# Segment sums of a graph network scanned and stored chunk by chunk, with one row per partition mended at the end

## What is computed

```python
def spline_conv(x, edge_index, basis, wi, weight, root, bias):   # twice, each behind elu
    msg = sum over s of basis[:, s, None] * xW[src, wi[:, s]]
    out = jax.ops.segment_sum(msg, dst, num_segments=n)
    deg = jax.ops.segment_sum(jnp.ones((dst.shape[0],)), dst, num_segments=n)
    out = out / jnp.clip(deg, 1.0)[:, None]
    return out + x @ root + bias

for l in range(3):                                               # layer 3
    e = edge_attr @ We[l] + be[l]
    msg = jax.nn.relu(x[src] + e)
    agg = jax.ops.segment_sum(msg, dst, num_segments=n)
    x = jax.nn.leaky_relu((x + agg) @ W[l] + b[l], negative_slope=0.01)
```

## Time and profile before

| | us |
|---|---|
| median of three runs | 7850.94 |
| profiled execution, own time | 7858.02 |
| its span | 7856.2 |
| DVE busy | 4300.7 (55%) |
| POOL busy | 5213.5 (66%) |
| PE busy | 2708.5 (34%) |
| ACT busy | 1275.8 (16%) |

### The profile page before, as it was taken

One profiled execution on the slowest core, in us unless ns is written; L12 is line 12 of the kernel. 1 busy time (PEld: TensorE's weight loads), 2 busy tenths in 40 slices (PEclk: granted clock), 3 DMA queues, 4 the chain that ended last, 5 costly groups with the idle time before them and its releaser, 6 DMA issues. The chain is left out here.

```text
span 7856.2 us, 39070 instructions
## 1 busy us (share of the span) xinstructions
PE 2708.5 (34%) x8375; PEld 1703.4 (22%) x8375; DVE 4300.7 (55%) x7258; ACT 1275.8 (16%) x2189; POOL 5213.5 (66%) x5106
## 2 busy tenths in 40 slices
PE   0000000005323300287745552776233365365222
PEld 0000000003211100133323332554133133233111
DVE  6999979921244700255548887778666422322311
ACT  0000000001111200276621010111244011011000
POOL 4777778887777277775567772663477476476477
PEclk9999999966555655698867776777555555555555
DMA  1111110013333000112212221221344222222111
GB/s 45 24 31 27 26 23 19 18 21 104 98 51 49 13 23 23 30 43 53 47 40 42 42 41 46 33 33 23 79 78 75 56 39 37 57 40 35 59 35 30
DMA packets 364618, 331.80 MB, mean 42 GB/s; under 512 B 115499, under 2 KB 339968, under 8 KB 363379
## 3 DMA queue, kind: packets, MB, share of 16 engines
q0 software_dynamic: 163072, 77.69, 11.5%
q1 hardware_dynamic: 199282, 249.37, 9.6%
q10 hardware_dynamic: 2048, 2.41, 0.1%
HBM read 173.11 MB, written 158.67 MB: 42 GB/s over the span
## 5 line engine op out<-in xcount | busy, mean ns | idle before, releaser
L889 POOL DMA_INDIRECT c_ring<-tab,QB x784 | 762.6, 973 | 614.5 <-POOLq L102 298.9
L889 POOL DMA_INDIRECT g_ring<-tab,QB x784 | 743.3, 948 | 420.4 <-issue 238.4
L889 POOL DMA_INDIRECT l_ring<-in_x_dram,a_own x392 | 538.4, 1373 | 130.9 <-issue 119.2
L1338 POOL DMA_INDIRECT nodes<-l1s_rowr,a_out x392 | 386.2, 985 | 264.3 <-DVE l1s_rowr L1354 145.1
L2007 POOL DMA_INDIRECT out_dram<-out_rowr,out_idxr x392 | 386.4, 986 | 221.9 <-issue 123.3
L1461 PE MATMUL c_psU<-spline,c_hzT 96*128 96x288 f32 x1568 | 516.8, 477 | 40.5 <-DVE c_V L1425 40.2
L889 POOL DMA_INDIRECT sort_ring<-in_x_dram,sort_raw x392 | 412.7, 1053 | 120.5 <-issue 119.2
L889 POOL DMA_INDIRECT l_ring<-agg_tab,QA x392 | 401.7, 1025 | 135.3 <-issue 119.2
L889 POOL DMA_INDIRECT H<-xe_tab,idx_a x392 | 406.0, 1036 | 122.6 <-issue 118.9
L889 POOL DMA_INDIRECT rows_b<-b_edges,idx_b x392 | 399.4, 1019 | 130.5 <-issue 118.9
L889 POOL DMA_INDIRECT c_ring<-nodes,b_other x392 | 386.9, 987 | 128.7 <-issue 118.0
(11 more groups left out here) (480 smaller groups left out, 8291.5 us busy)
## 6 DMA issues: line engine op xcount, KB each, us to landing
tab<-M SPq DMA_DIRECT2D x5, 6272.0 KB
nodes<-l_xout SPq DMA_DIRECT2D x40, 322.3 KB
nodes_x<-nodes SPq DMA_DIRECT2D x50, 257.8 KB
c_din<-dst_lin SPq DMA_DIRECT2D x98, 128.0 KB, 2.8
c_ring<-tab,QB POOLq DMA_INDIRECT x784, 3.3
dst_lin<-c_yd SPq DMA_DIRECT2D x98, 128.0 KB
g_din<-dst_lin SPq DMA_DIRECT2D x98, 128.0 KB, 2.8
g_ring<-tab,QB POOLq DMA_INDIRECT x784
```

Source lines behind the costliest of these rows:

```text
L889: pool.indirect_dma_start(out=ring[:, at + j, :], out_offset=None, in_=table, in_offset=bass.IndirectOffsetOnAxis(ap=idx[:, w:w + 1], axis ...
L1338: pool.indirect_dma_start(out=g.nodes2, out_offset=bass.IndirectOffsetOnAxis(ap=A.out[:, w:w + 1], axis=0), in_=rowr[k % NR][:, j, :], in_ ...
```

## The change

Nothing of what the reference computes is changed. Six edits:

1. **Scan within the stage.** A class `Segments` replaces `M`. The messages of chunk c go to a tile `T` of 128 x 32 x 9, feature by feature; column 0 takes the running sum of the chunk before (`open`), and two scans of 144 elements, 16 features each, sum the chunk (`scan`), with flags `B.run` laid out in the same form (made by ACT during c1). ACT copies `T` back to row order (`flatten`), and SP stores the chunk to the table (`keep`).
2. **Mending.** The sums of a partition's first segment lack what comes from the partitions before. Only the last row of that segment in each partition is used by the index lists, so at a stage's end one indirect DMA gathers 128 rows, DVE adds the carry (`close`), and one indirect DMA scatters them back (`mend`). `close_segments` is gone.
3. **The destination side** is loaded from the table by SP, chunk by chunk (128 KB each), in c2, c3, g0, g1 and out. In c2 and c3 it lands in the second half of `ring`, so that two additions of 256 elements become one of 512; the SP load then also waits for `tn.used`.
4. **Degree and bias.** `inv` goes into the spline's weights in `Basis`; the bias is a 97th row of the spline's weight matrix, against a row of ones in `hzT`. 18 small DMAs load it.
5. **The degree** is made in `l1s` instead of in layer 0, spread to every edge of a segment, along with the row numbers for the mending (`degrees`, `seams`), behind the eighth chunk.
6. Five tables instead of two, with their extra row stored in `l1s`.

```diff
 def load_weights(g, a):
+            bias = a["L2_gnn_b1"] if c == 0 else a["L2_gnn_b2"]
+            for j in range(9):
+                loads.append((g.spline[c][3 * D:3 * D + 1, j, :], bias.unsqueeze(0)))
 def layer0_edges(...):
-            link(v.memset(inv[:, :, :], 1.0))
-            scan_sum(g, v, link, ci, 0, inv, B, 1)
-            link(v.reciprocal(inv[:, :, :], inv[:, :, :]))
 def layer1_rest(...):                     # phase l1s, DVE
+            def degrees():
+                notlast = first
+                link(v.memset(count[:, :, :], 1.0))
+                scan_sum(g, v, link, ci, 0, count, B, 1)
...
+                carry_dve(v, link, cb, 0, [count[:, 0, :]], [sfx[:, 0:1]], back=True)
...
+                link(v.reciprocal(inv[:, :, :], count[:, :, :]))
             for k in range(g.NCH):
                 cols = slice(k * CH, (k + 1) * CH)
+                if k == 2 * NR:
+                    degrees()
+                    seams()
-def close_segments(g, B, M, table, ph_name, scale=None, bias=None):
...
+class Segments:
+    def into(self, c):
+        return self.T[c % self.n][:, :, 1:CH + 1].rearrange("p f w -> p w f")
+
+    def open(self, v, link, c):
+        if c >= self.n:
+            v.wait_ge(self.flat, c - self.n + 1)
+        if c == 0:
+            link.inc(v.memset(self.T[0][:, :, 0], 0.0))
+        else:
+            v.wait_ge(self.summed, 2 * c)
+            link.inc(v.tensor_copy(self.T[c % self.n][:, :, 0], self.T[(c - 1) % self.n][:, :, CH]))
+
+    def scan(self, v, link, c):
+        v.wait_ge(link.sem, link.base + link.n)
+        on = self.B.run[:, c, :, :].rearrange("p f w -> p (f w)")
+        for h in range(2):
+            t = self.T[c % self.n][:, h * (D // 2):(h + 1) * (D // 2), :].rearrange("p f w -> p (f w)")
+            v.tensor_tensor_scan(t, on, t, 0.0, ALU.mult, ALU.add).then_inc(self.summed, 1)
+
+    def flatten(self, act, c):
+        act.wait_ge(self.summed, 2 * (c + 1))
+        if c >= 2:
+            act.wait_ge(self.kept[c % 2], 16 * (c // 2))
+        act.copy(self.rows[c % 2][:, :, :], self.into(c)).then_inc(self.flat, 1)
+
+    def keep(self, sp, c):
+        sp.wait_ge(self.flat, c + 1)
+        sp.dma_start(lin(self.g, self.table[0:self.g.NP, :], c), self.rows[c % 2][:, :, :]).then_inc(self.kept[c % 2], 16)
+
+    def close(self, v, link):
+        g, last = self.g, self.T[(self.g.NCH - 1) % self.n]
+        v.wait_ge(self.summed, 2 * g.NCH)
+        carry_dve(v, link, self.c, 0, [last[:, :, CH]], [self.B.pfx[:, g.W - 1:g.W].broadcast_to([P, D])])
+        v.wait_ge(self.fetched, 16)
+        v.tensor_tensor(self.ends[:, :], self.ends[:, :], self.c.carry[:, :], ALU.add).then_inc(self.fixed, 1)
+
+    def mend(self, pool):
+        g, B = self.g, self.B
+        for i in range(2):
+            pool.wait_ge(self.kept[i], 16 * ((g.NCH + 1 - i) // 2))
+        pool.indirect_dma_start(out=self.ends[:, :], out_offset=None, in_=self.table,
+                                in_offset=bass.IndirectOffsetOnAxis(ap=B.get[:, 0:1], axis=0)).then_inc(self.fetched, 16)
+        pool.wait_ge(self.fixed, 1)
+        pool.indirect_dma_start(out=self.table, out_offset=bass.IndirectOffsetOnAxis(ap=B.put[:, 0:1], axis=0),
+                                in_=self.ends[:, :], in_offset=None, bounds_check=g.NP - 1, oob_is_err=False).then_inc(self.put, 16)
+        pool.wait_ge(self.put, 16)
 class Spline:                             # weigh, DVE
         times(0)
         times(1)
+        self.seg.open(v, link, c)
         add(0)
...
         add(3)
+        v.wait_ge(self.added, 4 * (c + 1))
+        self.seg.scan(v, link, c)
 def conv2_edges(...):
-                gather_from(g, pool, table, QB, ring[c % NR], c, 0, got[c % NR])
+                gather_from(g, pool, table, QB, ring[c % NR], c, 0, got[c % NR])
+            seg.mend(pool)
             def load(c):                  # SP
                 if c >= NR:
                     sp.wait_ge(tn.turned, c - NR + 1)
+                    sp.wait_ge(tn.used, c - NR + 1)
                 sp.dma_start(din[c % NR][:, :, :], lin(g, g.dst_lin, c)).then_inc(dgot[c % NR], 16)
+                sp.dma_start(ring[c % NR][:, CH:N2, :], lin(g, table[0:g.NP, :], c)).then_inc(mgot[c % NR], 16)
             def store(c):                 # SP
                 sp.wait_ge(new, c + 1)
                 sp.dma_start(lin(g, g.dst_lin, c), yd[c % 2][:, :, :]).then_inc(kept[c % 2], 16)
+                if c:
+                    seg.keep(sp, c - 1)
                 if c + 2 < g.NCH:         # ACT
                     tn.flatten(act, c + 2)
+                if c:
+                    seg.flatten(act, c - 1)
-                    link.inc(v.tensor_tensor(agg[:, 0:CH, :], pd[:, 0:CH, :], ring[c % NR][:, :, :], ALU.add))
-                    link(v.tensor_tensor(agg[:, CH:N2, :], pd[:, CH:N2, :], M[:, cols, :], ALU.add))
+                    link(v.tensor_tensor(agg[:, :, :], pd, ring[c % NR][:, :, :], ALU.add))
 class EdgeTerm:                           # message, DVE, in c3, g0, g1
+        seg.open(v, link, c)
...
-        link(v.tensor_scalar(M[:, cols, :], mm[:, :, :], 0.0, None, ALU.max))
+        link.inc(v.tensor_scalar(seg.into(c), mm[:, :, :], 0.0, None, ALU.max))
+        seg.scan(v, link, c)
 class Basis:
+        link(v.tensor_tensor(WT[:, :, 0, :], WT[:, :, 0, :], over(self.inv[:, cols, 0], 2, 3), ALU.mult))
```

More of the change, by code:

```diff
@@ L1323, in _ @@
             carry_pe(g, pe, c, 0)
+            carry_pe(g, pe, ci, 0)
+            carry_pe(g, pe, cb, 0, back=True)
         @block.sync
         def _(sp):
+            for i, t in enumerate(g.tabs):
+                sp.dma_start(t[g.NP:g.NP + 1, :], g.cbias[0:1, i, :] if i < 2 else g.zerow[0:1, 0:D]).then_inc(alone, 16)
             for k in range(g.NCH):
@@ new lines, with __init__ @@
+class Segments:
+    def __init__(self, ph, g, B, table, bank=None):
+        self.g, self.B, self.table, self.n = g, B, table, 3
+        self.T = [ph.sb(f"T{i}", [P, D, CH + 1]) for i in range(self.n)]
+        self.rows, self.kept = ph.sb2("rows", [P, CH, D]), ph.sem2("seg_kept")
+        self.ends = ph.sb("ends", [P, D])
+        self.summed, self.flat, self.fetched, self.fixed, self.put = (
+            ph.sem("seg_" + n) for n in ("summed", "flat", "fetched", "fixed", "put"))
+        self.c = carry_tiles(ph, D, bank)
+    def into(self, c):
[38 more added lines that the diff above has]
+        pool.wait_ge(self.put, 16)
@@ L1546, in _ @@
             link = Link(v, lk)
+            sp_.fill(v)
             for c in range(g.NCH + 1):
```

213 lines of the change are left out of this document (128 added, 85 removed).

## The result

The changed kernel takes 7642.84 us (median of four runs, 7635.39 to 7647.76); the kernel before, run beside it, 7838.82 us (four runs, 7818.64 to 7851.61). The ratio is 0.9745, 95% interval 0.9727 to 0.9762: 2.5% faster. The prediction was 7631 us, in a range of 7545 to 7735. The profiled execution of the changed kernel takes 7644.09 us, its span is 7642.3 us.

A forecast was written before the change was run, and what follows sets the result against it. DVE, waiting for PE once a chunk, bounds c1 and c2, POOL's gathers c3, g0, g1 and out. Closings of 444.6 less 225 us added give 220: 7858 becomes 7638, median 7631 us, range 7545 to 7735.

The forecast's parts named there:

- The closings: Between stages c1 to g1 and the next: last DVE instruction to first gather, five times, 444.6 us in all, goes.
- The tails: Chain of copy, store, mending and barrier at five stage ends: 11.4 us each, 61 us in all, 50 to 75.
- my row of 2.8: Trace's median landing time of c_din's DMA, 2.8 us, used for the tails' store and c2's load.
- The scans: In c1 and c2, DVE's two scans of 144 elements cost 0.83 us a chunk: 41 us in c1, 38 in c2.
- SP's queue in c2: SP waits for ACT's copy, so c_din loads a period late and PE stands 1.55 us in 46 chunks: 71 us.
- rival (c): TensorE's clock stays low in c1 and c2, DVE waits up to 1.4 us more a chunk: 137 us, 7768; chance 0.08.
- The stages that POOL sets: c3, g0, g1 and out: a busier DVE beside the gathers and out's third load cost 7 us, 0 to 25.
- Small parts: Weights' 18 more DMAs 5 us, Basis multiplications 2 us; degree's removal and new place, and the 97th row, nothing.
- (a): In c2 the load of c_din costs nothing: 71 us less than forecast, 7560 us; chance 0.20.
- (b) strided access: Writing T 36 bytes apart is charged on DVE: reductions 22 us, copies 10, tail 2; 7665 us; chance 0.22.
- (d), slower by gathers: In c3, g0 and g1 added work slows POOL's gathers; 0.19 us each uses up the gain; 8280 us; chance 0.03.
- The sum: Whole kernel: 444.6 us gone less 225 us of added terms, a gain of 220 us.

The follow-up runs named there:

- e10_drain_too: Changed kernel with SP's loads ahead of the store and ACT's copy ahead of exp in c2, 2 bias DMAs, early POOL DRAIN: 7571.48 us, ratio 0.9659.
- the execution with 750 us: Changed kernel without the mending's gather, addition and scatter; its profiled execution, 7624.84 us, had c2 at 750 us; median 7595.58 us, ratio 0.9700.

## Why the prediction was right, point by point

**The closings** were 445.5 us against 444.6. Nothing of them came back elsewhere.

**The tails** were mis-sized: 85 us, outside the 50 to 75 given. The step that failed is "the barrier (0.9 us on DVE, as ahead of the scans, and 0.7 more until POOL issues)". Both numbers came from barriers at which POOL had long been done. The missing term is POOL's DRAIN: 4 x 6.75 + 2.83 = 29.8 us. Less it, 55.3 stay, and with an early DRAIN 55.7 were measured. Of the smaller parts, the store was dearer in the forecast (0.4 + 2.8 us; the gather starts 2.0 us after ACT's copy has ended, SP's issue included). The Trainium skill (DMA: Bandwidth & Descriptors, Anatomy of one DMA) gives 2.0 us plus the bytes at 436 GB/s for a DMA that GpSimd issues, an estimate of 2.3 us for 128 KB. The store is SP's, but that estimate was nearer to this trace than my row of 2.8.

**The scans.** c1 +40.5 us against 41. The doubling gives 0.66 us a chunk, so 32.5 us of it; the wait of DVE on PE didn't shrink (68.8 us in 49 times, 71.5 before). The other 8 us were not taken apart. They are not the opening copy's.

**SP's queue in c2.** The mechanism is shown twice, by SP's order and by ACT's. The size was 40 us in this pair of traces, not 71. PE waited 45 times, as forecast (46), but 1.17 us on average and not 1.55, and beside these 52.6 us stand the 40.5 that c2 got shorter. Not all of the 40.5 need be the wait itself: `psU`'s matmuls took 480 ns on average in the changed kernel and 465 with the load in time.

```profile
L1541 PE MATMUL c_psU<-spline,c_hzT 97*128 97x288 f32 x784 | 259.8, 480 | 19.8 <-DVE c_V L1501 19.7
```

**What the forecast of c2 lacked** is 63 - 36 = 27 us that neither order takes away. Rows of PE's matmuls in c2, before and in the run with ACT's copy early (columns: busy us, mean ns):

```profile
L1461 PE MATMUL c_psU<-spline,c_hzT 96*128 96x288 f32 x764 | 231.1, 440 | 23.7 <-DVE c_V L1425 23.7
L1450 PE MATMUL c_psT<-ident,c_hz 128*96 128x128 f32 x392 | 97.6, 398 | 14.2 <-DVE c_hz L1415 11.0 <-ACT c_hzT L1471 2.8
```

```profile
L1541 PE MATMUL c_psU<-spline,c_hzT 97*128 97x288 f32 x776 | 250.6, 465 | 23.4 <-DVE c_V L1501 23.4
L1528 PE MATMUL c_psT<-ident,c_hz 128*96 128x128 f32 x392 | 105.3, 424 | 12.9 <-DVE c_hz L1491 11.4 <-ACT c_hzT L1551 1.5
```

Each matmul is 25 ns longer with the same columns, and `psT`'s have the same shape in both kernels, so the 97th row isn't the reason. The granted clock over 500 us of c2 is 0.79 before and 0.75 in this run and in e10_drain_too, and PE had stood longer before each chunk's root product (164.0 us in all instead of 128.3, 3.5 a chunk instead of 2.7, since DVE's scans come in between). DVE's wait for `psU` rose from 1.99 to 2.38 us a time, 19 us over the stage. This is rival (c), with a seventh of its price (19 of 137 us). It is read from rows; no run held the clock fixed, and the last 8 us, like those of c1, were not taken apart. In the forecast 71 stood where 40 + 27 belong, so that c2 came out right (103 against 109) by two errors; by the execution with 750 us it would have been 126.

**The stages that POOL sets** grew by 27 us, not 7, just outside the 0 to 25. A gather of g0 went from 948 to 970 ns on average. Neither DVE's work (scans doubled: no growth) nor the load of `own` (4 ns for two) does it. In the five other kernels on chips like the first, g0 took 506.4 to 508.7 us, so a part of the 10 us is this execution's. What makes the other 5 us a stage stays open. The store of the rows, the other DMA that g0 has more, and ACT's copy weren't left out.

**Small parts.** The first gather of the sort came 4.7 us later (5 forecast). The degree's removal and new place: nothing, as forecast.

**The rivals.** (a) is what the two orders make of the kernel: 7593.58 and 7600.29 us, where (a) said 7560; c2's other 27 us are the larger part of the rest, and the forecast was itself 12 us under the changed kernel's median. (b) strided access: the reductions into `T`, 36 bytes apart, against those into `M` before (min, median, max in ns):

```profile
L1507 DVE TENSOR_REDUCE c_T<-c_V x392: 1110/1131/1154, 4033.0 to 5499.6; 128x64 f32<-128x576 f32 x196
```

```profile
L1432 DVE TENSOR_REDUCE M<-c_V x392: 1097/1128/1144, 4057.9 to 5470.7; 128x64 f32<-128x576 f32 x196
```

3 ns, where the rival had 0.22 us for the four of a chunk, 55 ns each: it is wrong for DVE's reductions. ACT's copy may pay one: 256 elements out of `T` take 653 ns, 256 out of PSUM 372 (`out_aT`) and an exp of 512 side by side in SBUF 630 (`c_e`). The forecast had 0.4. No run laid `T` out side by side, so that the distance of 36 bytes is the reason is not shown. The Trainium skill's rule that an access to a new 16-byte line is charged (SBUF — State Buffer, Door 1: The DMA port swizzle) doesn't show in the reductions and could be what the copy shows. (d), slower by gathers: 22 ns a gather, a ninth of the 0.19 us that would have used up the gain.

**The sum** was off by 6 us in 214 between the profiled executions; between the medians 196 us were gained, against 220 forecast. The 6 us were luck too: tails +24, POOL's stages +20, c2 -6, and -32 ahead of c1, of which 17 are TensorE's clock in the stage of all nodes, which the change barely touches, and 11 layer 0, which differs as much between two executions of the kernel before.

## What to carry to other kernels

Put a store that waits for one engine behind the loads in the issuing queue, or make what it waits for come first: 40 us of 7640 hung on two lines, and both cures gave the same. Before a barrier comes onto the path, read the queue instructions of the engine that gathers: a DRAIN of 6.6 us was in the trace before, hidden, and a DRAIN placed where another engine still works took 29 us from five tails. A sum that comes out right proves none of its terms; each was to be measured by itself.

## What was unexpected of the hardware

POOL's DRAIN ends 6.6 us after the last gather of c2, c3, g0 and g1, and takes 0.21 us if a DRAIN has come ahead of the last two indirect DMAs. Waiting doesn't shorten it. At the end of c1 and of c2 in the changed kernel POOL had stood 55 and 59 us before its last two indirect DMAs, and the DRAIN took 2.83 and 6.75 us:

```profile
4762.32 0.95 POOL L1451 DMA_INDIRECT c_ends<-tab,b_get  x1 [55.44 <-DMA tab<-c_rows]
...
L98 POOLq DRAIN  x1: 2826/2826/2826, 4770.3 to 4770.3; - x1
```

```profile
5504.20 0.94 POOL L1451 DMA_INDIRECT c_ends<-tab,b_get  x1 [59.44 <-DMA tab<-c_rows]
...
L98 POOLq DRAIN  x1: 6750/6750/6750, 5510.8 to 5510.8; - x1
```

The early DRAIN of e10_drain_too, right behind c1's gathers, ends 2.84 us after the last of them, at 4701.7:

```profile
4697.71 1.15 POOL L891 DMA_INDIRECT c_ring<-nodes,b_other  x1 [0.30 <-issue]
...
L1448 POOLq DRAIN  x1: 11158/11158/11158, 4690.5 to 4690.5; - x1
```

So the price goes with the stage and not with the idle time. c1's last gathers read `nodes` and the others' `tab`; whether that is the reason stays open.

On two of the chips every kernel took 1600 us more. The instructions are as long as elsewhere (reductions 1133 ns), but in g0 ACT, DVE and PE all stand for 9 to 11 us every few chunks, with nothing in the records that releases them, while POOL goes on. From g0 in the run with the early copy of the rows:

```profile
7907.98 0.94 POOL L892 DMA_INDIRECT g_ring<-tab,QB  x1 [0.30 <-issue]
7909.23 0.95 POOL L892 DMA_INDIRECT g_ring<-tab,QB  x1 [0.30 <-issue]
7909.50 0.59 ACT L2076 COPY g_e<-g_psD 128x512 f32<-128x512 f32 x1 [11.32 <-DMA c_din<-dst_lin]
...
7910.12 0.43 DVE L2100 SCALAR_TENSOR_TENSOR S<-g_e 128x256 f32<-128x256 f32 x1 [9.70 <-issue]
...
7912.65 0.50 PEld L1857 LDWEIGHTS g_psE<-we,g_eT 104*128 104x128 f32 x2 [9.02 <-issue]
```

The releaser named for ACT belongs to an earlier stage, so it isn't one. The cause is open. The same kernel (ACT's copy early) saved 198 us against the one before there, and 239 on a chip without the stalls, so these chips' ratios are not set beside the others'.
